# Macaron block (half FFN, linear attention, half FFN) on one core: every engine's list written out anew, free banks for scores and sums, a second DMA queue for one move

## What is computed

```python
def ln(x): return (x - mean(x)) / sqrt(var(x) + 1e-5)
def ffn(x): return relu(x @ W1 + b1) @ W2 + b2            # 128 -> 512 -> 128
def attn(x):                                              # 8 heads of 16, blocks of 32 tokens
    q, k, v = split(x @ w_qkv.T)
    qp = elu(q_head @ proj_head) + 1                      # 16 -> 128 features per head
    kp = elu(k_head @ proj_head) + 1
    num = qp @ (kp.T @ v)   within each block of 32
    z = 1 / (qp @ sum(kp) + 1e-8)
    return (num * z) @ w_out.T + b_out
x = x + 0.5 * ffn(ln(x))      # FFN a, normalisation 0
x = x + attn(ln(x))           # normalisation 1
x = x + 0.5 * ffn(ln(x))      # FFN b, normalisation 2
```

## Time and profile before

| | us |
|---|---|
| median of 3 runs (lowest, highest) | 146.1 (144.58, 146.41) |
| the profiled execution's own time | 146.55 |
| its span in the profile | 144.5 |
| mean granted clock of PE | 0.953 |

### The profile page before, as it was taken

One profiled execution on the slowest core, in us unless ns is written; L12 is line 12 of the kernel. 1 busy time (PEld: TensorE's weight loads), 2 busy tenths in 40 slices (PEclk: granted clock), 3 DMA queues, 4 the chain that ended last, 5 costly groups with the idle time before them and its releaser, 6 DMA issues.

```text
span 144.5 us, 4470 instructions
## 1 busy us (share of the span) xinstructions
PE 118.5 (82%) x1889; PEld 93.8 (65%) x1889; DVE 94.1 (65%) x258; ACT 77.9 (54%) x125; POOL 57.7 (40%) x90
## 2 busy tenths in 40 slices
PE   5888989887599797899627998998599869962992
PEld 5776957854288564498415675986458837961991
DVE  3699883384685996774995874798874933038311
ACT  4256472487673789546545598665688110701540
POOL 3319277449980491000099900069500091007000
PEclk9999999999999999999985699999999995999699
DMA  4986920640065000092000065000100020000202
GB/s 120 271 231 100 182 48 0 260 176 0 5 253 187 2 5 5 11 346 82 0 7 7 0 223 217 5 5 25 52 0 5 0 73 5 0 0 0 73 5 73
DMA packets 10651, 11.03 MB, mean 76 GB/s; under 512 B 772, under 2 KB 6920, under 8 KB 10632
## 3 DMA queue, kind: packets, MB, share of 16 engines
q1 hardware_dynamic: 10480, 10.49, 23.4%
q10 hardware_dynamic: 152, 0.26, 0.7%
HBM read 2.36 MB, written 1.05 MB: 24 GB/s over the span
## 4 chain that ended last, share of the span: by engine, by line
PE 34%; DVE 25%; issue 15%; ACT 12%; POOL 9%; DMA 3%; POOLq 1%
PE G L302 9%; DVE stats L758 6%; ACT expo L625 6%; DVE feat L794 6%; PE G L308 4%; POOL rstd L977 3%; ACT hidden L610 3%; DVE mean_var L762 3%; PE G L277 3%; DMA x_in<-in_L_attn_x_dram 3%; PE SO L302 2%; PE wide L323 2%; POOL xn L989 2%; POOL v_blocks L1036 2%; DVE xn L777 2%
## 5 line engine op out<-in xcount | busy, mean ns | idle before, releaser
L794 DVE SCALAR_TENSOR_TENSOR feat<-expo,wide 128x1024 f32<-128x1024 f32 x32 | 37.6, 1217 | 13.6 <-ACT expo L625 13.5
L625 ACT ACTIVATE expo<-wide,minus_one 128x1024 f32<-128x1024 f32 x32 | 33.9, 1114 | 15.4 <-PE wide L323 15.4
L977 POOL TENSOR_TENSOR rstd<-var_eps,minus_half 128x4 f32<-128x4 f32 (+1 forms) x15 | 13.5, 898 | 52.9 <-DVE minus_mean L766 52.9
L302 PE MATMUL G<-w,hidden 128*128 128x128 f32 x192 | 23.3, 277 | 0.0
L302 PEld LDWEIGHTS G<-w,hidden 128*128 128x128 f32 x192 | 22.1, 192 | 0.2
L323 PE MATMUL wide<-qk_packed,proj_packed 64*128 64x512 f32 x64 | 12.2, 460 | 9.8 <-DVE feat L794 9.2
L277 PE MATMUL G<-ident,xn 128*128 128x128 f32 x48 | 11.3, 328 | 7.0 <-DVE xn L777 5.3
L610 ACT ACTIVATE hidden<-G,b_cols 128x512 f32<-128x512 f32 (+1 forms) x22 | 13.7, 667 | 5.0 <-PE G L294 5.0
L1036 POOL TENSOR_SCALAR v_blocks<-v_rows,own_block 128x544 f32<-128x544 f32 x16 | 11.5, 739 | 8.8 <-ACT v_rows L621 8.8
L323 PEld LDWEIGHTS wide<-qk_packed,proj_packed 64*128 64x128 f32 x64 | 5.0, 192 | 15.3 <-DVE feat L794 9.6
L601 ACT CAST xnT_hi<-G 128x512 fp32r<-128x512 f32 (+1 forms) x10 | 5.0, 505 | 16.7 <-PE G L277 16.7
(11 more groups left out here) (96 smaller groups left out, 206.8 us busy)
## 6 DMA issues: line engine op xcount, KB each, us to landing
qk_packed<-qk_hi SPq DMA_DIRECT2D x16, 256.0 KB, 2.6
qk_packed<-qk_lo SPq DMA_DIRECT2D x8, 256.0 KB, 4.3
qk_packed<-sixteenth SPq DMA_DIRECT2D x2, 512.0 KB, 8.1
x_in<-in_L_attn_x_dram SPq DMA_DIRECT2D x3, 256.0 KB, 5.3
out_dram<-x SPq DMA_DIRECT2D x3, 256.0 KB, 2.3
proj_rows<-in_L_attn_proj_dram SPq DMA_DIRECT2D x6, 64.0 KB, 2.8
x_in<-in_L_attn_x_dram SPq DMA_DIRECT2D x2, 128.0 KB, 3.6
w<-in_L_ffn_W_dram ACTq DMA_DIRECT2D x1, 256.0 KB, 3.5
```

Of the source, the lines that this page charges most:

```text
L302: mm = pe.matmul(bank[:, t * D:(t + 1) * D], hidden[f][:, i, (t0 + t) * P:(t0 + t + 1) * P], w2[:, i, :], start=(i == 0 and t == 0), stop= ...
L625: nc.scalar.activation(expo[:, n % 2, :, :], wide[n % 2][:, :, :], ACT.Exp, bias=minus_one[:, 0:1]).then_inc(exp_done, 1)
L794: nc.vector.scalar_tensor_tensor(out=feat[:, n % 4, :, :], in0=expo[:, n % 2, :, :], scalar=1.0, in1=wide[n % 2][:, :, :], op0=ALU.min, op ...
L977: nc.gpsimd.tensor_tensor(rstd[k][:, at], var_eps[k][:, at], minus_half[:, 0:unit[2]], ALU.pow).then_inc(rstd_ready[k], 1)
```

## The change

- `episode`, `step` and the fillers go. Each engine's list is written out call by call, in an order of its own; `ffn_down` and `turn_normed` can be cut into parts, and a feature product now waits for one feature only (its own double bank).
- Scores and sums of a pair no longer lie in SO: `score_pair`, `mix_pair`, `scores_copy` and `divide` take a bank, each time one of SO, GA, GB, GC (late ones W0B, W1A, W1B) that is free. The waits of `mix_pair` on the divide before and of `divide` on the next scores copy are gone from the helpers; hand-over waits of whole banks stand in the PE list instead.
- In chunk 0, ACT issues the second move of the high part itself, right after copying it (`move_again`); SP issues the other two.
- At the start PE turns the first tile as soon as it is there, and the ten warm-ups are spread between the turns of units 0 to 2 and the turning of the weights. DVE sets `proj_rows` only after the statistics of all five units of x; the statistics of units 2 and 3 come ahead of `w1_low`.
- FFN b of chunk 1 (unit 1) is mostly behind the last pair; FFN b's units 2, 3 and 4 are interleaved with it and with each other.

```diff
@@ SP
+            def move_qk(c, g, term):
+                source, ready = (qk_lo, qk_lo_ready) if term == LO_HI else (qk_hi, qk_hi_ready)
+                wait(sp, ready, 2 * c + g + 1)
+                wait(sp, feat_sum, HEADS * (c - 2) + HALF * (g + 1) if c >= 2 else 0)
+                sp.dma_start(qk_packed[term::TERMS, c % 2, g * HALF:(g + 1) * HALF, :].bitcast(F32),
+                             source[:, g, :].bitcast(F32)).then_inc(qk_moved[g], 16)
...
+            load_proj(1, HI_LO)
+            load_bout()
             move_ones(0)
             move_ones(1)
-            move_qk(0)
+            move_qk(0, 0, HI_HI)
+            move_qk(0, 0, LO_HI)
+            move_qk(0, 1, HI_HI)
+            move_qk(0, 1, LO_HI)
+            move_qk(1, 0, HI_HI)
+            move_qk(1, 0, HI_LO)
+            move_qk(1, 0, LO_HI)
...
@@ PE, helpers
-            def episode(m):
-                wait(pe, feat_ready, 2 * m + 2)
-                if m + 1 < NPAIRS:
-                    feature_product(2 * m + 2)
-                    feature_product(2 * m + 3)
-                if m:
-                    mix_pair(m - 1)
-                score(2 * m)
-                score(2 * m + 1).then_inc(scored, 1)
+            def score_pair(m, bank):
+                wait(pe, feat_ready, 2 * m + 2)
+                score(2 * m, bank)
+                score(2 * m + 1, bank).then_inc(scored, 1)
...
             def mix_pair(m, bank):
                 wait(pe, scores_out, m + 1)
-                wait(pe, attn_ready, m)
...
@@ PE, the start
-            for _ in range(WARMUP):
-                pe.matmul(GC[:, 0:P], ident[:, :], ident[:, :], start=True, stop=True)
+            turn_normed(0, 0, 0, 1, GA)
+            warm_up(GB)
+            turn_weights(GC)
+            for _ in range(2):
+                warm_up(GB)
+            turn_normed(0, 0, 1, 2, GA)
+            turn_normed(0, 1, 0, 1, SO)
+            for _ in range(5):
+                warm_up(GB)
+            turn_normed(0, 1, 1, 2, SO)
+            turn_normed(0, 2, 0, 1, W0A)
+            for _ in range(2):
+                warm_up(GB)
+            turn_b1(W0B)
+            turn_normed(0, 2, 1, 4, W0A)
+            up_high(0, 0, 0, GB)
...
@@ PE, pairs 4 to 6
+            score_pair(4, GB)
+            pe.wait_ge(feat_ready, 11)
+            feature_product(12)
+            pe.wait_ge(hidden_ready[0], 19)
+            out_product(0, GC)
+            pe.wait_ge(attnT_ready, 1)
+            up_high(0, 4, 3, GA)
+            up_low(0, 4, 3, GA)
+            pe.wait_ge(scores_out, 5)
+            turn_normed(1, 3, 0, 4, GB)
+            pe.wait_ge(x2_ready, 1)
+            mix_pair(4, GC)
+            pe.wait_ge(hidden_ready[0], 20)
+            score_pair(5, GA)
+            pe.wait_ge(feat_ready, 12)
+            feature_product(13)
+            pe.wait_ge(feat_ready, 13)
+            feature_product(14)
...
@@ PE, the end
+            pe.wait_ge(feat_ready, 32)
+            score_pair(15, W1A)
+            pe.wait_ge(attn_ready, 14)
+            turn_normed(2, 2, 0, 3, GC)
+            up_low(1, 1, 1, GB)
+            mix_pair(15, W1B)
...
+            turn_attn(3, GB)
+            ffn_down(1, 1, 1, 2, GA)
...
+            ffn_down(1, 3, 3, 4, GA)
+            ffn_down(1, 4, 0, 1, SO)
+            up_low(1, 4, 3, GB)
+            ffn_down(1, 4, 1, 4, SO)
@@ ACT
+            def move_again(c, g):
+                wait(act, qk_hi_ready, 2 * c + g + 1)
+                act.dma_start(qk_packed[HI_LO::TERMS, c % 2, g * HALF:(g + 1) * HALF, :].bitcast(F32),
+                              qk_hi[:, g, :].bitcast(F32)).then_inc(qk_moved[g], 16)
...
-            act.wait_ge(pool_set, 1)
-            nc.scalar.mul(minus_one[:, :], minus_half[:, 0:1], 2.0).then_inc(minus_one_set, 1)
-            act.wait_ge(w_loaded[W_W1], 16)
-            nc.scalar.copy(w1_hi[:, :], w1[:, :]).then_inc(w1_hi_ready, 1)
             normed_hi(0, 0, GA)
+            w1_high()
+            normed_hi(0, 1, SO)
...
+            proj_rounding()
+            qk_hi_copy(0, 0, SO)
+            move_again(0, 0)
             normed_hi(0, 3, GB)
+            relu(0, 2, 3, W0B)
+            v_copy(0, W1B)
+            qk_hi_copy(0, 1, W1A)
+            move_again(0, 1)
@@ DVE
-                wait(dve, scores_out, min(m + 2, NPAIRS))
...
-            nc.vector.memset(proj_rows[:, :, :], 1.0).then_inc(rows_set, 1)
+            find_mask()
+            find_own_block()
+            norm_stats(0, 0)
+            norm_stats(0, 1)
+            norm_apply(0, 0, 0, 1)
+            norm_stats(0, 2)
+            norm_apply(0, 0, 1, 2)
+            norm_apply(0, 1, 0, 2)
+            norm_stats(0, 3)
+            w1_low()
             normed_lo(0, 0, GA)
+            normed_lo(0, 1, SO)
+            norm_stats(0, 4)
+            set_rows()
+            normed_lo(0, 2, W0A)
...
+            feature(7)
+            feature(8)
+            divide(2, GA)
+            divide(3, GB)
+            feature(9)
...
+            divide(12, GB)
+            feature(29)
+            attn_residual(2, GB)
+            norm_stats(2, 2)
+            feature(30)
+            feature(31)
+            divide(13, GC)
+            divide(14, W0B)
+            ffn_b_residual(0, SO)
+            divide(15, W1B)
```

More of the change, by code:

```diff
@@ new lines, in _ @@
+            exp(9)
+            exp(10)
+            relu(0, 4, 2, GC)
+            attn_copy(0, GA)
+            exp(11)
+            exp(12)
+            scores_copy(4, GB)
+            relu(0, 4, 3, GA)
+            normed_copy(3, GB)
+            scores_copy(5, GA)
+            exp(13)
+            qk_hi_copy(2, 0, GB)
+            exp(14)
+            exp(15)
+            qk_hi_copy(2, 1, GC)
+            v_copy(2, GA)
+            scores_copy(6, SO)
+            exp(16)
+            scores_copy(7, SO)
@@ new lines, in _ @@
+            exp(17)
+            normed_hi(2, 0, GB)
+            exp(18)
+            attn_copy(1, SO)
+            normed_copy(4, GA)
+            exp(19)
+            exp(20)
+            scores_copy(8, GC)
+            qk_hi_copy(3, 0, SO)
+            exp(21)
+            exp(22)
+            scores_copy(9, GC)
+            v_copy(3, SO)
+            relu(1, 0, 0, GA)
+            qk_hi_copy(3, 1, GB)
+            exp(23)
+            scores_copy(10, SO)
+            exp(24)
+            relu(1, 0, 1, GA)
@@ new lines, in _ @@
+            scores_copy(11, GA)
+            exp(25)
+            exp(26)
+            relu(1, 0, 2, GA)
+            normed_hi(2, 1, GC)
+            scores_copy(12, GA)
+            exp(27)
+            exp(28)
+            attn_copy(2, GB)
+            relu(1, 0, 3, GA)
+            exp(29)
+            relu(1, 1, 0, GC)
+            scores_copy(13, GA)
+            exp(30)
+            scores_copy(14, GA)
+            exp(31)
+            scores_copy(15, W1A)
+            relu(1, 1, 1, GB)
@@ L968, in _ @@
[L968 removed]
+            normed_lo(0, 4, GC)
+            feature(2)
+            feature(3)
+            ffn_a_residual(3, GB)
+            norm_stats(1, 3)
+            feature(4)
+            divide(0, GC)
+            qk_lo_part(1, 0, GA)
+            feature(5)
+            feature(6)
+            qk_lo_part(1, 1, GC)
+            divide(1, GA)
+            feature(7)
[3 more added lines that the diff above has]
+            feature(9)
@@ new lines, in _ @@
+            feature(18)
+            normed_lo(2, 0, GB)
+            feature(19)
+            feature(20)
+            qk_lo_part(3, 0, SO)
+            attn_residual(1, GA)
+            divide(8, GB)
+            feature(21)
+            feature(22)
+            norm_stats(2, 1)
+            qk_lo_part(3, 1, GB)
+            feature(23)
+            feature(24)
+            divide(9, GC)
+            divide(10, GB)
+            feature(25)
+            feature(26)
+            divide(11, GB)
```

1184 lines of the change are left out of this document (665 added, 519 removed).

## The result

The changed kernel takes 126.61 us (median of 4 runs, 125.44 to 127.82) against 146.25 for the one before, measured beside it: a ratio of 0.866, interval 0.853 to 0.880. The forecast was 132.0; the direction was right, the size of the gain was not: 19.6 us in place of 14.1. (Medians are of all executions; ratios, and where the text says "counted", leave out those more than 1.5% above the fastest of the same kernel.) The profiled execution took 127.23 us with a span of 125.4.

What follows compares the result with a forecast made beforehand. PE bounds the start; in the middle no engine is full, the product-exp-feature loop and fillers leaving idle time; the tail is a chain. 146.55 + 3 (start) - 9.6 (middle) - 7.4 (tail) = 132.5, so 132.0 us; range 127 to 142.

Steps and rivals of the forecast that it cites:

- the release by both features: Middle, old kernel: PE issues the next two feature products only after both features of a pair; not priced alone.
- the long filler: Middle, old kernel: behind FFN down, 3.77 us from start to start, ACT and DVE run dry; not priced alone.
- I take +3: Start, up to the first feature: DVE's new order makes it 3 us later, bounds +1 and +7.
- late feeds: Rival: x or ones land late, start costs 6, middle takes 76, tail 25.5; 141.1 us in all, chance 0.23.
- The queue edit: Start, chunk 0: ACT issuing the second move saves only issue time; put at 0, bounds -1.2 and +1.2.
- I add 3 and take 71: Middle: 3 us added to the walk's 68 for unlucky meetings and half clock; 71 us, 9.6 less than before.
- The walk: Middle: all four lists followed from 32 us, 0.2 us per hand-over; 68 us from first to last feature.
- 66 (DVE 93% full): Middle: lower bound of 66 us from first to last feature, against an upper bound of 80.6.
- About 6 us lost: Old kernel, three half-clock stretches behind thin PE work: some 12 us of work at half clock, about 6 us lost.
- the stretch at 78 us: Middle: half clock near 78 us expected not to come in the new kernel; 2.3 of the 9.6 us gained.
- The pace stays: Rival: middle keeps 80.6 us, start costs 3, tail gives 5; 144.1 us in all, chance 0.09.
- Series: Rival: the two double banks don't overlap, each feature takes 3.1 us; 161 us, chance 0.06 with the like.

Runs made afterwards that it cites:

- start_early: The changed kernel with proj_rows set first again and the old kernel's start (ten warm-ups first, turns of two tiles at once): 124.31 us.
- start_early_2: The same kernel as start_early (changed kernel, proj_rows first, old start), run again for an interval: 123.58 us, ratio 0.842 to the old kernel.
- both_features: The changed kernel, but every even feature product from number 2 on waits for both features of the pair before: 159.6 us, ratio 1.087.
- old_warm: The old kernel with warm-up products, their results unused, in four thin stretches of PE: 143.93 us, ratio 0.989.

## Why the prediction was right in kind and short in size

**The bound.** Right: the idle time was in the middle and in the tail. The middle gave 14.4 us and the tail 8.1. Right too: ACT and DVE waited in the loop of product, exp and feature, 28.3 us before and 9.5 after. But the two causes that the forecast named for it, the release by both features and the long filler, are worth 2.0 and some 0.6 us when they alone are taken out of the old lists. The hand-overs mix, divide, scores copy, mix through the one bank SO were named in half a sentence and never priced. Putting them back in the new lists costs 4.5, 8.2 and, together, 11 to 13 us, though the middle of the old trace has no wait for them. How the 14.4 us of the middle divide between free banks, release and order stays open: the three work through each other, and no run frees the banks in the old order.

**The start.** "I take +3": it was +3.4. FFN a began at 13.70 (14.2 forecast), the first feature at 35.41 (34 to 36). It came from the written order of the start, as start_early and start_early_2 show; the late feeds had at most about 1 us of it. The queue edit "at 0" measured 0. The Trainium skill (DMA: Bandwidth & Descriptors, "Issuing engines are not separate DMA queues") had allowed only the time to issue to be saved, and the run agrees: 126.07 us without the second queue, 126.61 and 126.5 with it. The Trainium skill has the table load right before the ACTIVATE that needs it (ScalarE: Activation LUTs, "Step-by-step: what each stage is for"), from which the prediction made up to 0.5 us. The load stayed at 1.85 us although the copy behind it waited until 10.66, so that this half microsecond did not arise.

**The middle.** Here is the failing step: "I add 3 and take 71". The walk gave 68 and the trace 66.2. Of the 4.8 us that were too much, 3 were the allowance, added because 67.4 of busy PE had once become 80.6, and 1.8 the walk itself. The walk's features 11, 15, 20, 26 and 31 were to end at 56.6, 67.2, 77.1, 90.5 and 101.6, with the first feature begun at 33.6, 1.8 us ahead of the real one. They ended at about 58.9, 68.9, 78.4, 90.9 and 101.6: late by 2.3 at first, level at the end. The allowance stood for unlucky meetings and for a half clock; the trace of the changed kernel has a clock of 1.00 in the middle, and its longest single wait in the loop is 1.5 us. The old ratio of 67.4 to 80.6 belonged to the old order, which the walk had already replaced. The lower bound, "66 (DVE 93% full)", is what came: DVE is busy 60.5 of 66.2 us, 91%, and PE even 64.0, where the forecast had summed 62.5. The low end of the range had a middle of 67 and a tail of 23.3, 124.9 us with a start of +1, and was then lifted to 127 because all three at once seemed unlikely. The middle and the tail both came out near that end, at 66.2 and 23.8, and only the start didn't.

**The half clock.** "About 6 us lost" in the old kernel looks too high. The prediction priced the stretch at 78 us at 2.3 us, half its length, and put that much of the middle's gain down to it. Full clock at this place gave features 20 and 21 1.2 us, since PE then has 0.6 of 2 us idle there; a new half-clock stretch near 103 us took them again. There is a second sign, a correlation only: of 30 executions of the kernel before beside these runs, the six at a mean clock of 0.939 or 0.940 took 147.2 us on average and the fifteen at 0.961 to 0.965 took 145.2. That is 2.0 us for a mean clock lower by 0.025, which over 145 us is 3.6 us of PE's full speed. Both say about half of what the prediction reckoned. What all three stretches cost was not measured. That the new kernel doesn't fall to 0.50 in the middle was right.

**The tail.** 24.5 forecast, 23.8 measured; 2.7 us from the last residual's start to the end, as before. One swap in the old list gives 4 to 5 of the 8 us; the rest is put down to the interleaving, which no run tests.

**The rivals.** Late feeds: fell, the start cost 3.4 and not 6, and earlier feeds gained nothing that could be measured. The pace stays: fell. Series: fell, with 9.5 us of loop waits; both_features shows that it was a real danger, 159.6 us for the 161 of the forecast, though at another clock.

**The sum.** Against the profiled executions: start +0.4, middle -4.8, tail -0.7, around the span -0.2 make -5.3, from 132.5 to 127.23.

## What to carry to other kernels

Two small tiles in one bank forbid orders. The middle of the trace before shows no wait at either hand-over, and in the order that free banks allow, putting both back costs 11 to 13 us of 126.5. So ask of a shared bank what it keeps you from writing, and not only what it makes an engine wait for. Single edits of a written order don't add up and can't be read backwards: the same release was worth 2 us in an order that didn't use it and 33 in one that was built on it, and the 11 to 13 us of the hand-overs are of the second kind. With PE busy 97% of a stretch, waits and a late start passed nearly one to one to the end (3.7 us of waits cost 4.5, a first feature 3.5 us earlier gave 3.4). A walk of all lists by hand came within 1.8 us of 66.2; what failed was the allowance carried over from the kernel that it replaced. And look at the whole trace after an edit: full clock at one place had moved the half clock to another.

## What was not expected of the hardware

- In the first 7 us the column of the granted clock reads 1.00, yet the warm-ups take 0.23 us each (20 in 4.64 us). The same instruction takes 0.117 in the middle of old_warm. Either the column is wrong at the start or something else slows the products there; no run tells which. The row of old_warm, at a granted clock of 1.00:

```profile
72.76 3.51 PE L499 MATMUL G<-ident 128*128 128x128 f32 x30
```

- Two profiles of the kernel with the old start show 0.58 and 0.56 at 8 to 12 us in the one and 1.00 in the other. Their counts say that the column is right here: from 8 to 12 us the first has 23 instructions of PE, the second 35. The first feature followed at 32.77 and at 31.42. First start_early, then start_early_2:

```profile
8.00:10.00 2.00, 1.81 (x10) 1.71 (x9) 1.97 (x10) 0.47 (x3) 1.92 (x2) 0.58 0.92 235
10.00:12.00 2.00, 2.00 (x13) 2.00 (x12) 1.90 (x16) 1.75 (x4) 1.44 (x3) 0.56 0.41 91
```

```profile
8.00:10.00 2.00, 1.81 (x16) 1.65 (x14) 1.97 (x9) 1.00 (x4) 1.48 (x2) 1.00 1.07 278
10.00:12.00 2.00, 2.00 (x19) 2.00 (x18) 1.90 (x17) 1.02 (x4) 1.67 (x3) 1.00 0.42 95
```

- Products whose results nobody reads kept the clock at 1.00 where they stood, and a half-clock stretch came up later, near 103 us, in a place where the old kernel had none.
